# First two blocks' weight turning and product order, and two loads of x moved ahead of a store, in a four-stage residual chain

## What is computed

```
ctx   = ema(x, tau)                                   # h = alpha*h + x_t along the sequence
gated = x * sigmoid([x, ctx] @ Wg.T + bg)
h1    = gelu(x @ Wn1.T + bn1);  mod = 0.5 + sigmoid(h1 @ Wn2.T + bn2)
temporal = sum_d softmax(blend)_d * ema(gated * mod_d, tau_d)          # d = 0, 1
gate  = sigmoid(temporal @ Wtemp.T + btemp);  soma = gelu(x @ Wsoma.T + bsoma)
x = x + layernorm((soma * gate) @ Wout.T) * gamma + beta               # stage 0
x = x + x @ W[cat] + b[cat]                                            # stage 1
x = x + layernorm(x + relu(x @ W1 + b1) @ W2 + b2) * gamma2 + beta2    # stage 2
x = x + x @ W3.T + b3                                                  # stage 3
```

## Time and profile before

| what | value |
|---|---|
| median of 3 runs | 810.23 us (810.14 to 812.13) |
| the profiled execution, its own time | 812.93 us |
| its span, first to last instruction | 811.1 us |
| mean granted TensorE clock | 0.992 |
| PE busy | 777.3 us (96%), 3628 matmuls |
| weight loads (PEld, beside PE) | 632.4 us (78%) |
| DVE, ACT, POOL busy | 534.0 (66%), 324.2 (40%), 101.4 us (13%) |
| DMA | 66.29 MB, mean 82 GB/s |

### The profile page before, as it was taken

The page is one execution under the profiler, slowest core; times in us unless marked ns, Lnnn a source line. Parts: engine busy times, 40 slices in busy tenths (PEclk is TensorE's granted clock), DMA queues, the critical chain, the costliest instruction groups (busy, mean ns, idle before and its releaser), DMA issues. The chain is left out here.

```text
span 811.1 us, 10802 instructions
## 1 busy us (share of the span) xinstructions
PE 777.3 (96%) x3628; PEld 632.4 (78%) x3628; DVE 534.0 (66%) x782; ACT 324.2 (40%) x525; POOL 101.4 (13%) x227
## 2 busy tenths in 40 slices
PE   5996999999999999999999999997999999999997
PEld 4785788788788788788788788876888888888886
DVE  2496596577477577568469469656676667666655
ACT  3343414414414413522512612646544545436331
POOL 2000003003003003003003003523010020110100
PEclk9998999999999999999999999999999999999999
DMA  7412102201200300400400512534241322313102
GB/s 228 148 53 84 47 1 68 91 25 47 108 26 31 124 26 0 155 26 0 155 26 0 152 59 87 198 130 156 79 155 40 116 105 77 131 40 129 39 27 79
DMA packets 32480, 66.29 MB, mean 82 GB/s; under 512 B 10800, under 2 KB 11824, under 8 KB 30400
## 3 DMA queue, kind: packets, MB, share of 16 engines
q1 hardware_dynamic: 32224, 65.87, 23.7%
q0 software_dynamic: 224, 0.00, 0.0%
HBM read 40.67 MB, written 25.20 MB: 81 GB/s over the span
## 5 line engine op out<-in xcount | busy, mean ns | idle before, releaser
L555 PE MATMUL pc<-x_h,wg_h 128*128 128x512 f32 x224 | 89.7, 400 | 1.6 <-ACT wg_h L923 1.6
L557 PE MATMUL pc<-x_h,wg_l 128*128 128x512 f32 x224 | 88.8, 396 | 0.0
L556 PE MATMUL pc<-x_l,wg_h 128*128 128x512 f32 x224 | 87.9, 393 | 0.0
L1282 DVE TENSOR_TENSOR_SCAN stage_b<-alpha,carry,stage_b 128x512 f32<-128x512 f32 x64 | 78.5, 1268 | 0.0
L1217 DVE TENSOR_TENSOR x_l<-x_t,x_h 128x512 fp32r<-128x512 f32 x32 | 22.2, 692 | 63.9 <-ACT x_t L938 63.9
L988 ACT ACTIVATE ctx_t<-ctx_t,col_bg 128x512 f32<-128x512 f32 x32 | 23.2, 724 | 97.2 <-DVE ctx_t L1262 97.2
L647 PE MATMUL pm<-t_h,wt_h 128*128 128x512 f32 x128 | 53.0, 414 | 3.7 <-issue 3.6
L555 PE MATMUL pm<-wo_h,s_h 128*128 128x512 f32 x128 | 50.6, 396 | 0.7 <-DVE s_l L1241 0.7
L649 PE MATMUL pm<-t_h,wt_l 128*128 128x512 f32 x128 | 51.3, 400 | 0.0
L555 PEld LDWEIGHTS pc<-x_h,wg_h 128*128 128x128 f32 x224 | 42.6, 190 | 11.1 <-ACT wg_h L923 1.8
L648 PE MATMUL pm<-t_l,wt_h 128*128 128x512 f32 x128 | 51.0, 399 | 0.0
(11 more groups left out here) (226 smaller groups left out, 1888.6 us busy)
## 6 DMA issues: line engine op xcount, KB each, us to landing
xt_scratch<-x_t SPq DMA_DIRECT2D x8, 1024.0 KB, 4.1
n_scratch<-stage_a SPq DMA_DIRECT2D x8, 1024.0 KB, 4.9
ctx_t<-xt_scratch SPq DMA_DIRECT2D x16, 512.0 KB, 6.3
x_tok<-in_x_dram SPq DMA_DIRECT2D x30, 256.0 KB, 4.3
out_dram<-x_tok SPq DMA_DIRECT2D x28, 256.0 KB, 2.0
s_h<-n_scratch SPq DMA_DIRECT2D x12, 512.0 KB, 4.8
mod<-mod_scratch SPq DMA_DIRECT2D x8, 512.0 KB, 3.5
stage_b<-in_L_cond_weight_dram SPq DMA_DIRECT2D x2, 1024.0 KB, 5.4
```

The source lines that it names most:

```text
L555: nc.tensor.matmul(acc, ah, bh, start=start and q == 0, stop=False)
L556: nc.tensor.matmul(acc, ah, bl, start=False, stop=False)
L557: last = nc.tensor.matmul(acc, al, bh, start=False, stop=stop and q == n - 1)
L1282: nc.vector.tensor_tensor_scan(tr[:, m % 2, :], alpha[:, 1 + d:2 + d].to_broadcast([P, BLK]), tr[:, m % 2, :], carry[:, D - d, m:m + 1], A ...
```

## The change

It changes order alone; no arithmetic is added or left out.

- SP: the raw Wn1 is loaded after two tiles of x instead of after four. In `step`, the loads of tiles 2 and 3 of the next block stand ahead of `store_n`.
- PE, block 0: Wn1 is turned between tiles 1 and 2 of x; `h1_product(0)` is cut in two halves of six matmuls, and the turning of WGC stands between them. WGX chunks 1 and 2 are turned together behind u chunk 1, chunk 3 behind u chunk 2, none behind u chunk 3. ACT and DVE follow; ACT's `mod_tanh(0)` moves ahead of the copies of chunks 1 and 2.
- Block 1: Wout is no longer turned ahead of the first temp product, but after u chunk 3 of block 1, and PE waits for it only ahead of `out_product(0, 0)`. The temp products of block 0 are cut otherwise: chunk 0, tiles 2 and 3 of x, chunk 1, h1, u chunks 0 and 1, chunks 2 and 3, mod. ACT and DVE are reordered to fit; a wait of PE for `gate_t` is added ahead of the turning of Wout, since both use `pm`.

```diff
-        BEHIND_U = [[(WGX, [0])], [(WGX, [1])], [(WGX, [2])], [(WGX, [3])]]
+        BEHIND_U = [[(WGX, [0])], [(WGX, [1, 2])], [(WGX, [3])], []]
...
-            for j in range(TILES):
-                load_x(0, j)
+            load_x(0, 0)
+            load_x(0, 1)
             load_weight(WN1)
+            load_x(0, 2)
+            load_x(0, 3)
             load_weight(WGC)
...
                 spread_mod(i)
-                store_n(i - 1)
                 load_x(i + 1, 2)
                 load_x(i + 1, 3)
+                store_n(i - 1)
...
-            def h1_product(i):
+            def h1_product(i, between=None):
                 pe.wait_ge(xcopy, i * TILES + TILES)
                 pe.wait_ge(xlo, i * TILES + TILES)
-                product(pt[0][:, :], of_x(wn1_h, wn1_l, 0, slice(0, H))).then_inc(h1_mm, 1)
+                pairs = of_x(wn1_h, wn1_l, 0, slice(0, H))
+                product(pt[0][:, :], pairs[:2], stop=False)
+                if between:
+                    between()
+                product(pt[0][:, :], pairs[2:], start=False).then_inc(h1_mm, 1)
...
-            def step_end(i):
+            def step_end(i, first=False):
                 for m in range(NC):
                     v_chunk(i, m)
+                if first:
+                    ready(WOUT)
                 for k in range(TILES):
                     out_product(i - 1, k)
...
-            for k in range(TILES):
-                turn_x(0, k)
+            turn_x(0, 0)
+            turn_x(0, 1)
             prepare(WN1, [0])
+            turn_x(0, 2)
+            turn_x(0, 3)
             ready(WN1)
-            h1_product(0)
-            prepare(WGC, range(NC))
+            h1_product(0, lambda: prepare(WGC, range(NC)))
...
             next_x(0)
-            prepare(WOUT, range(NC))
-            ready(WOUT)
-            temp_product(0, (0, 1))
+            ready(WTEMP)
+            temp_product(0, (0,))
             turn_x(1, 2)
             turn_x(1, 3)
+            temp_product(0, (1,))
             h1_product(1)
             u_chunk(1, 0)
             u_chunk(1, 1)
+            temp_product(0, (2, 3))
             mod_product(1)
-            temp_product(0, (2, 3))
             u_chunk(1, 2)
             u_chunk(1, 3)
-            step_end(1)
+            pe.wait_ge(gate_t, NC)
+            prepare(WOUT, range(NC))
+            step_end(1, first=True)
...
             hidden(1)
             temporal_hi(0, 2)
-            mod_tanh(1)
             temporal_hi(0, 3)
-            gates(0)
+            gates(0, lambda: mod_tanh(1))
+            prepare(WOUT, range(NC))
             traces_part(1)
...
             blend_traces(0, 1)
             x_lo_part(1, 0)
-            prepare(WOUT, [0, 1])
+            temporal_lo(0, 1)
             x_lo_part(1, 1)
-            prepare(WOUT, [2, 3])
-            temporal_lo(0, 1)
-            scan_traces(0, 2)
             modulate(0, 3)
             x_lo_part(1, 2)
             x_lo_part(1, 3)
+            scan_traces(0, 2)
             blend_traces(0, 2)
             scan_traces(0, 3)
-            hidden_lo(1)
             temporal_lo(0, 2)
             blend_traces(0, 3)
+            hidden_lo(1)
+            temporal_lo(0, 3)
             scan_context(1, 0)
-            temporal_lo(0, 3)
             scan_context(1, 1)
             gates(0)
             scan_context(1, 2)
             scan_context(1, 3)
+            prepare(WOUT, range(NC))
             traces_part(1)
```

More of the change, by code:

```diff
@@ L1030, in step @@
                 traces_part(i, last)
-            for k in range(TILES):
-                copy_x(0, k)
+            copy_x(0, 0)
+            copy_x(0, 1)
             prepare(WN1, [0])
+            copy_x(0, 2)
+            copy_x(0, 3)
             prepare(WGC, range(NC))
@@ L1040, in _ @@
             prepare_behind(BEHIND_U, 0)
+            mod_tanh(0)
             prepare_behind(BEHIND_U, 1)
-            mod_tanh(0)
             prepare_behind(BEHIND_U, 2)
-            prepare_behind(BEHIND_U, 3)
             for m in range(NC):
@@ L1351, in _ @@
             nc.vector.memset(keep[:, 0:1], 0.0).then_inc(setup_v, 1)
-            for k in range(TILES):
-                x_lo_part(0, k)
+            x_lo_part(0, 0)
+            x_lo_part(0, 1)
             prepare(WN1, [0])
+            x_lo_part(0, 2)
+            x_lo_part(0, 3)
             prepare(WGC, range(NC))
```

## The result

The changed kernel takes **787.55 us** (median of 4 runs, 786.92 to 788.74), the kernel before 811.18 (4 runs, 810.14 to 813.63, three of them the runs of the first table): ratio 0.9706, 95% interval 0.9679 to 0.9733, 2.9% faster. The forecast was 788.7, its range 785.0 to 793.0. The profiled execution took 787.42 us, 25.5 less than the profiled 812.93 of before. Against that pair the sum of the forecast, 21.5, was 4.0 short.

The account below looks back on a forecast made before the run. PE was taken as the bound, busy 96% of the span, losing time only to waits and the lower clock. 9.5 + 1.8 + 11.3 - 1.1 = 21.5 us off the profiled 812.93 gave 791.4, against the median 810.23 788.7; range 785.0 to 793.0.

Parts of the forecast that it names:

- Loads ahead of the store: Loop steps: x loads issued before the store remove PE's wait for tile 2, about 1.68 us a step, 9.5 us over six.
- WGX: Block 0 ahead of v0: last chunk turned behind u2, so u3 covers its copies; 1.8 us gained.
- Block 1: From the turning of block 1's x to v0: idle times and half clock go, 11.3 us gained.
- The sum of PE's own work: Block 1, turning of x to v0: products, turned pieces and changes of kind take 29.2 us if no wait is left.
- The new waits: Block 1: the `gate_t` wait costs nothing; `out_product` asks for Wout only after four v chunks.
- Start: Block 0 up to u0: transposes cutting the h1 products keep the clock from rising, 1.1 us lost.
- rival 1: Block 0 start: the clock rises in spite of the transposes, start gains 1.3, total 786.3 us; chance 0.30.
- the good case, 1.3: Block 0 start: all else equal, u0 would begin at 19.1 instead of 20.47, 1.3 us gained.

Follow-up runs that it names:

- experiment 10: The kernel of experiment 9 with Wn1 again loaded and turned behind all four tiles of x: 787.45 us.
- experiment 6: The changed kernel with Wn1 loaded, turned and split behind all four tiles of x again, the cut in h1 kept: 785.63 us.
- experiment 7: The changed kernel with the h1 product in one piece and WGC turned behind it: 789.55 us.
- experiment 2: The kernel before with only the two loads of x moved ahead of the store: 801.72 us.
- experiment 3: The changed kernel with block 1 in its old order, Wout turned ahead of the temp products, temp chunks 0 and 1 together: 799.0 us.
- experiment 4: The changed kernel with block 0 in its old order (Wn1 last, h1 in one piece, one WGX chunk behind each u chunk): 788.92 us.
- experiment 8: The changed kernel with the turning of block 0's normalised tiles 12 products later in the second pass, on PE alone: 789.9 us.
- experiment 9: The kernel of experiment 8 with ACT and DVE also splitting the first l1 chunk ahead of the normalisation: 786.31 us.

## Why the prediction was right, and where not

- **Loads ahead of the store: right** in place and size. The forecast was 9.5, the table has 9.49, the run that takes this part away gave 10.5, and the one that has it alone 9.95. A step is 60.56 us from one turning to the next, 1.69 less than the 62.25 of before (1.68 forecast).
- **WGX: right**, 1.80, and 1.7 when undone.
- **Block 1: right**, 11.65 for 11.3, and 11.2 when undone. The sum of PE's own work came 0.35 too long. The new waits, for `gate_t` and for Wout ahead of `out_product`, show no idle time, and neither does anything else in the stretch.
- **Start: wrong in sign.** The step that failed is "I take -1.1: in both places that the trace shows, the products ran on unbroken until the rise". From two rises behind products I took that the rise needs them. The measured gain is 1.09, and rival 1 holds. Sixteen transposes between the products kept the clock from rising in no profile: the second half of h1 was at full clock in all, seven of which began h1 at the lower level. Here PE did nothing but turn pieces for 2.2 us (3.3 in experiment 10) and came out of it at full clock. The Trainium skill ("TensorE: Matmul & The Clock Gate", Part 4: PE-mode transpose) says that the full clock does not engage for transposes. The trace does not agree: in six profiles the first product of h1 was already at full clock, and PE had executed nothing before it but twenty transposes, of float32 as all here. The forecast of the good case, 1.3, was nearly right: 0.3 lost to Wn1's place and some 1.4 won by the cut, by experiments 6 and 7. What one execution shows is still luck in part, as the start runs at either clock (see below): the old order at full clock had u0 at 18.66, 0.7 ahead of the new order at the lower one.
- **Missed: the clock's fall in the second pass.** The sum treated everything behind block 7 as fixed. It isn't: the same wait of 3.36 us costs 1.45 us more in one execution than in another. In this pair of profiles that adds 1.4 us to the difference; it is no effect of the change that any run shows.
- **The total came out closer than the terms allow.** The terms were short by 4.0 against the profiled pair: 2.2 in the start, 1.4 in the fall, 0.35 in block 1. The base was the median shown, 810.23, and the profiled execution of before had been 2.7 us longer than that. The miss of the time, 788.7 - 787.55, is only 1.15, and that is luck: between the medians of the result the difference is 23.6 us, 2.1 more than the sum of the terms, and the base was 0.95 too low, which made up for part of it.

## What to carry to other kernels

A load behind a store in one queue waits for what the store waits for, and here it landed later too (5.0 us after issue instead of 2.8), so the load whose buffer comes free first goes first. An idle gap of PE can cost more than its length (1.8 times in block 1), since the half clock behind it is a cost of its own: price a gap by the distance between two fixed points around it, not by its row among the waits. To cover a gap, follow the chain to the engines that free the banks: by the medians, moving PE's order alone lost 2.4 us here, while moving the turning together with ACT's and DVE's splits of both chunks won 2.8.

## What the runs showed of the hardware

- **The same start runs at either clock.** In six profiles (experiments 2, 3, 4, 6, 7 and 8) the first product of h1 already ran at full clock; in the eight others, before and after among them, the first six to nine ran at 0.43 us. From the first h1 product to u0, with the cut, it was 5.36 us in the first kind and 6.65 to 7.72 in the second. Neither the order of the start nor the time of that product (10.7 to 12.5 against 11.1 to 12.4) separates them. The mean granted clock of such a stretch is 1.00 even so (12.3 to 15.0 us in the changed kernel): at the start of an execution the distance of the products tells the clock, and the granted clock does not. Ahead of that first product PE had executed only twenty turned pieces, in both kinds at the price of the lower level, and then stood idle for 1.8 to 2.1 us. In experiment 6, ahead of its h1 at full clock:

```profile
3.62 1.94 PE L562 MATMUL pt<-ident,x_tok 128*128 128x128 f32 x8 [3.62 <-DMA x_tok<-in_x_dram]
6.41 1.97 PE L562 MATMUL pt<-ident,ctx_t 128*128 128x128 f32 x8 [0.85 <-DMA ctx_t<-in_x_dram]
8.17 1.06 PE L562 MATMUL pm<-ident,gate 128*128 128x128 f32 x4
```

- **The clock's fall behind an idle time is not a matter of its length alone.** In eight of ten profiles it fell behind the same 3.36 us and in two it did not; it fell behind 2.54 us in block 1, and behind 0.54 and 2.12 us in experiment 10, but not behind 0.52 and 2.10 in experiment 9.
- **The first loads land one to two us apart** in executions with the same order of loads: the pieces behind x's first pair were turned from 6.07 to 7.29 on in the five profiles with the old order, and from 5.38 to 7.54 on in the nine with the new one. With the two above this is of the size of the few us by which executions of one kernel differ; that it is their cause is not shown, as each kernel has one profile.
